# Local attention: ScalarE's two exponentials of a score tile queued behind two copies instead of directly behind the scores

## The reference, cut to what matters

```python
def local_attention(q, k, v):              # window w = 32, 16 heads of 64
    ...                                    # each block of 32 queries sees 64 keys:
    sim = jnp.einsum('bhwie,bhwje->bhwij', bq, bk2) * QK_SCALE
    sim = jnp.where(mask, -jnp.finfo(sim.dtype).max, sim)
    attn = jax.nn.softmax(sim, -1)
    out = jnp.einsum('bhwij,bhwje->bhwie', attn, bv2)

def attn_layer(x, Wqkv, qs, ksc, Wo):
    qkv = x @ Wqkv                         # 128 -> 3 * 1024
    q = l2norm(q) * qs;  k = l2norm(k) * ksc
    q = q * cos * scale + rotate_half(q) * sin * scale
    k = k * cos * inv + rotate_half(k) * sin * inv
    return local_attention(q, k, v) @ Wo

for i in range(6):
    x = attn_layer(shift_tokens(x), ...) + x
    x = ffn_layer(shift_tokens(x), ...) + x    # layer norm, gated gelu, 341 wide
```

## Time and profile before

| | |
|---|---|
| median of 3 runs | 4403.01 us (4397.09 to 4404.81) |
| profiled execution | 4397.26 us, span 4395.5 us |
| PE busy | 4212.1 us, 96% of the span |
| DVE, ACT, POOL busy | 3251.4, 2614.8, 2168.8 us |
| granted TensorE clock, mean | 0.99 |

### The profile page before, as it was taken

How to read it: one execution, slowest core, us unless ns; L and a number is a source line. 1 busy time by engine, 2 the same in 40 slices (tenths; PEclk the granted TensorE clock), 3 DMA queues, 4 the chain that set the end, 5 groups by cost and what they waited for, 6 DMA issues and landing times.

```text
span 4395.5 us, 159359 instructions
## 1 busy us (share of the span) xinstructions
PE 4212.1 (96%) x68360; PEld 2541.8 (58%) x68360; DVE 3251.4 (74%) x5759; ACT 2614.8 (59%) x5346; POOL 2168.8 (49%) x1986
## 2 busy tenths in 40 slices
PE   8999999999799999999999999999999999999998
PEld 4555555555356666556656656656656556656655
DVE  5666666565578887877887877878887877878875
ACT  4545555455366666666666666666666666666664
POOL 0000000000176766766766766766766666766763
PEclk9999999999899999999999999999999999999998
DMA  1000000000111112111121111211122111221112
GB/s 45 4 8 6 8 4 9 6 8 4 41 52 49 52 45 70 52 47 46 51 71 52 49 46 49 70 51 48 51 61 60 45 50 46 64 60 50 50 46 68
DMA packets 141403, 185.95 MB, mean 42 GB/s; under 512 B 32870, under 2 KB 63652, under 8 KB 140708
## 3 DMA queue, kind: packets, MB, share of 16 engines
q1 hardware_dynamic: 140708, 175.76, 14.7%
HBM read 26.76 MB, written 4.19 MB: 7 GB/s over the span
## 4 chain that ended last, share of the span: by engine, by line
PE 69%; issue 2%; ACT 1%; POOL 1%; DVE 1%; DMA 0%; SPq 0%; DVEq 0%; POOLq 0%; ACTq 0%
PE psum L1599 23%; PE psum L1540 9%; PE psum L1616 8%; PE psum L1604 8%; PE psum L1525 6%; PE psum L1637 6%; PE psum L1609 4%; PE psum L1642 3%; PE psum L1562 2%; PE psum L1622 1%; PE psum L1632 0%; ACT pT L1692 0%; ACT oTl L1694 0%; DVE cs L1779 0%; POOL cs L1480 0%
## 5 line engine op out<-in xcount | busy, mean ns | idle before, releaser
L1480 POOL TENSOR_TENSOR cs<-cs 128x512 f32<-128x512 f32 x768 | 975.7, 1276 | 489.8 <-DVE cs L1779 479.8
L1599 PE MATMUL psum<-wqkv,xw 128*128 128x512 f32 x2304 | 1172.6, 608 | 11.4 <-DMA wqkv<-in_wqkv 9.8
L1779 DVE TENSOR_TENSOR cs<-psum,rots 128x1024 f32<-128x1024 f32 x768 | 930.8, 1212 | 202.1 <-PE psum L1599 195.9
L1489 POOL TENSOR_TENSOR qk<-cs,rn 128x512 f32<-128x512 f32 x768 | 776.5, 1042 | 422.0 <-ACT rn L1663 422.0
L1676 ACT ACTIVATE sq<-psum 128x512 f32<-128x512 f32 x768 | 462.2, 602 | 512.6 <-PE psum L1609 178.7
L1508 POOL MEMSET tiled<- 128x128 bf16 x1 | 0.2, 205 | 1168.1 <-POOLq L590 1168.1
L1736 DVE TENSOR_REDUCE ss<-sq 128x8 f32<-128x512 f32 x768 | 519.4, 676 | 12.4 <-ACT sq L1676 0.8
L1604 PEld LDWEIGHTS psum<-ident,qk 128*128 128x128 f32 x3072 | 362.3, 142 | 219.0 <-issue 199.9
L1599 PEld LDWEIGHTS psum<-wqkv,xw 128*128 128x128 f32 x2304 | 370.8, 191 | 174.9 <-issue 132.5
L1540 PEld LDWEIGHTS psum<-pT,vw 64*64 64x64 f32 x18432 | 382.2, 135 | 110.5 <-issue 110.0
L1506 POOL TENSOR_TENSOR probl<-probl,rs 128x512 f32<-128x512 f32 x384 | 392.4, 1043 | 94.8 <-DVE rs L1769 92.5
(11 more groups left out here) (198 smaller groups left out, 6636.0 us busy)
## 6 DMA issues: line engine op xcount, KB each, us to landing
vw<-vl SPq DMA_DIRECT2D x768, 128.0 KB, 2.4
vw<-vl SPq DMA_DIRECT2D x672, 64.0 KB, 2.1
wqkv<-in_wqkv SPq DMA_DIRECT2D x36, 256.0 KB, 4.5
wol<-in_wol SPq DMA_DIRECT2D x6, 512.0 KB, 3.8
xin<-in_x SPq DMA_DIRECT2D x9, 256.0 KB, 2.9
xr<-in_x SPq DMA_DIRECT2D x8, 256.0 KB, 3.1
sums<-sumout SPq DMA_DIRECT2D x8, 256.0 KB, 2.3
cs<-sums SPq DMA_DIRECT2D x8, 256.0 KB, 4.5
```

Of the source, the lines that this page charges most:

```text
L1480: summed_rot.done(nc.gpsimd.tensor_tensor(own, own, halves(cs[:, t % 2, j, 1, :])[:, :, ::-1, :], ALU.add), at)
L1489: rotated.done(nc.gpsimd.tensor_tensor(qk[:, j, :].rearrange("p (h c) -> p h c", c=EL), cs[:, t % 2, j, 0, :].rearrange("p (h c) -> p h c" ...
L1599: last = nc.tensor.matmul(ps[:, :], xw[:, t * P:(t + 1) * P], wqkv[:, col:col + BANK], start=True, stop=True)
L1779: parts.done(V.tensor_tensor(cs[:, t % 2, j, :, :].rearrange("p i (h c) -> p i h c", c=EL), twice, by_head, ALU.mult), at)
```

## The change

A function `behind_copy` rewrites the list of keys for ScalarE alone. It takes the keys `s.t.0` and `s.t.1` out and puts them back behind the second copy (`t`, `pt`, `o` or `v`) that follows. Where an `n`, `w` or `gate` comes first, they are put back ahead of that. The lists of the other engines stay.

```diff
+def behind_copy(order, kinds, copies):
+    out, held, left = [], [], 0
+    for key in order:
+        if key[0] in kinds:
+            held.append(key)
+            left = copies
+            continue
+        if key[0] in ("n", "w", "gate"):
+            out, held = out + held, []
+        out.append(key)
+        if key[0] in ("t", "pt", "o", "v"):
+            left -= 1
+            if left <= 0:
+                out, held = out + held, []
+    return out + held
...
@@ block.scalar
             for it, order in enumerate(ORDERS):
-                for key in order:
+                for key in behind_copy(order, ("s",), 2):
                     read(it, key)
```

## The result

| | before | changed |
|---|---|---|
| median of 4 runs | 4400.05 us | 4479.91 us (4472.49 to 4481.57) |
| ratio | 1 | 1.018 (95% interval 1.0167 to 1.0193) |
| profiled execution, span | 4397.3, 4395.5 us | 4478.9, 4477.1 us |
| granted TensorE clock, mean | 0.99 | 0.99 |

The forecast was 4466 us with a range of 4425 to 4484 and a chance of 0.91 for slower. The changed kernel does the same work: the page counts the same instructions, and PE, DVE and POOL are busy as long as before to within 0.5%. The 80 us are waiting and pauses of PE. The page shows 64 us more idle time (183.4 before, 247.7 now) and 17 us more busy time; the ends of matmuls are modelled late, so a part of each wait counts as busy.

The account below looks back on a forecast made before the run. PE, busy for 96% of the span, was taken as the bound. Tile 0's 68 us, plus 2 for tile 3, less 3 of pauses, gave +67 us on 4397.3: 4464, predicted as 4466 us, range 4425 to 4484.

Parts of the forecast that it names:

- Tile 3: Two copies, v.0.1 and t.0.0, go ahead; first exponential 0.12 us late; cost 0 to 6 us, taken as 2.
- Tile 0: Exponentials 3.2 us late behind square qk.2.0 and copies v.1.1, t.1.0; reciprocal 2.30 us late; 68 us lost in all.
- First wait: PE at pt.0.0 waits 1.3 us for the first half of POOL's product, in two of three trips.
- Second wait: PE at the mask of tile 1 waits for ACT's kTl copy of t.1.3, 0.45 us in the typical trip.
- DVE's sums: DVE's sums wait for ACT's late exponentials: 2.3 us more idle time per trip, about 100 us in all.
- ACT's exponentials: ACT's idle time before its exponentials falls by about 2.5 us per trip, from 283 to some 165 us.
- The waits: PE's loss per trip: 2.55 us less the distance from kTl copy's end to tile 1's mask; together 68 us.
- The issue pauses: In tile 1's scores behind the mask, a semaphore wait lets PE skip issue pauses of 4.5 us; taken as -3.
- The earlier copies of tile 3: They leave about 1 us earlier; their banks go to o.2.1 and qk.1.3, where neither waits; gain 0.
- Rival 1: PE's issue pauses, about 40 us, are paid back by the waits; loss 28 us, 4425 us; chance 0.11.
- rival 2: No cover counts for PE's waits: 48 times 2.30 = 110 us, 4507 us; chance 0.05.
- Rival 3: Earlier copies of tile 3 free banks PE's mask waits on; at most 24.4 us gained, 4373 us; chance 0.04.

Follow-up runs that it names:

- e1: Kernel before, with only tile 3's exponentials put behind v.0.1 and t.0.0, tile 0's left in place: ratio 0.9992, -2.8 us.
- e2: Kernel before, with only tile 0's exponentials put behind qk.2.0, v.1.1 and t.1.0: ratio 1.0178, +79 us.
- e4: Kernel before, with tile 0's exponentials behind the square of qk.2.0 alone, ahead of both copies: ratio 1.0079, +37 us.
- e7: Kernel before, with ACT's copy of t.1.3 moved behind the square of qk.2.2: ratio 1.0093, +39 us.
- e6: Kernel before, with ACT's square of qk.3.1 moved behind the copies of t.2.3, o.0.0 and o.0.1: 4363.65 us, ratio 0.9918.
- e5: Kernel before, with tile 0's exponentials behind t.1.0 and DVE's sums of tile 0 behind the rotary product of qk.2.1: ratio 1.0105, +45.5 us.

## Why the prediction was right, and where its sum was off

**The mechanism held step by step.**
- Tile 3: first exponential 0.12 us late. From PE's start of s.3.0 to it, it was 2.80 us and is 2.91 (4028.52 to 4031.43). Cost: forecast 2 us (0 to 6), measured -2.8 us, with an interval that reaches to no change (e1).
- Tile 0: sums 2.30 us late. From PE's start of s.0.0 to the first sum, it was 4.41 us and is 6.70: 2.29 us.
- First wait 1.3 us: 1.31, in 27 of 47 trips where I had two of three. Second wait 0.45 us: 0.31.
- DVE's sums: 116.7 us of idle time for the forecast "about 100". ACT's exponentials: 186.7 for "some 165". Those of tiles 0 and 3 lost 111 us of idle time (118 forecast), and those of tile 1 gained 13, since the pauses of s.1.0 make them wait.
- The two exponentials together: I had 0.53 us from one start to the next, and the row of 1.17 us for two of 0.64 gives the same 0.53.
- Nothing later in the trip was paid twice, and nothing but tile 0 paid (e1, e2).

**Three terms of the sum were mis-sized.**
- *The waits: 68 forecast, 57 measured over the same 48 trips.* For the handover from ACT's copy to the mask I took 0.25 us from a place of the chain where the mask of tile 2 waits for pT. There it is 0.25 us in the typical trip too. But at tile 1, behind the copy of kTl, the mask of the changed kernel starts 0.14 us after the copy's end. Each trip so has 0.11 us more cover, 5 us in all. Of the other 5 us, 2.7 lie in trips 8, 21, 34 and 47, which had no pause in o.3 before and have one now, and so more cover; the rest is spread over trips with such a pause.
- *The issue pauses: -3 forecast, about +20 measured.* This is the step that failed in sign. I wrote that a wait "can let it skip an 'issue' pause right behind". The runs show the reverse at the scores of tile 1: +18.3 us in the changed kernel, +17.1, +16.9 and +17.2 in e2, e4 and e7, and -8.8 at tile 2 when the wait ahead of it is taken away (e6). What I described does exist: in e5, where PE waits at pt.0.0 and the mask's copy is in time, s.1.0 loses its 4.3 us. It fails where the awaited copy is the one that opens the score tile.
- *The earlier copies of tile 3: nothing forecast, -10.5 us measured in o.2.0, as a part of the +20.* I put the gain at 0 because no PE row waits for those banks. With the copy of v.0.1 2.8 instead of 0.8 us ahead of oa.2 the pauses of o.2.0 went, and 8.8 us came back in s.0.0, so that tile 3 still comes out near nothing.

The time lies 4 us inside the upper end of the range, and that 67 came so near to 80 is luck: the waits, sized 11 us too high, hid half of the 23 us by which the pauses were missed. The last step of the sum is also off. 4464 us for the profiled execution and the median's 5.7 us above it make 4470, and I wrote 4466.

Rival 1, the pauses paid back, didn't come: in all they grew; rival 2 (no cover) had the wrong reason for a larger loss. Rival 3, that earlier copies pay, was rightly put aside for this change, since it moves none of the copies that L1562 waits for. Its price, the 24.4 us, was there to be had all the same: e6 takes it by letting copies pass a square.

## What to carry to other kernels

Idle time in front of an instruction is a place for other work only if that work is ready then. An instruction which brings a wait of its own (here a square that waits for DVE) moves that wait ahead of everything put behind it, and the engine still idles. So look, item by item, at when each thing that goes ahead becomes ready, and at who waits for what goes behind: two copies ahead cost nothing, the same two with one square cost 1.8%. And where a busy PE comes to dense runs of short matmuls, what opens such a run should be ready well ahead: here 0.8 us ahead still left pauses, 1.5 us or more hardly any.

## What the runs showed of the hardware

A late copy costs PE twice: once as a wait, and again as a pause some 2.4 us further on, inside the run of 64 short matmuls, in the trips in which, as I read it, a block of its code ends there. Three things in the traces point to the supply of instructions. The page of the changed kernel has a queue for it,

```profile
q8 instruction: 549, 8.99, 0.8%
```

which is 549 packets of 16.4 KB, 477 of them in the local attention. First, the place of the pause moves by ten matmuls from one trip to the next: in the changed kernel it lies behind the 40th, 50th and 60th of the 64 in trips 1 to 3, then behind the 2nd, 12th and so on to the 62nd in trips 10 to 16. Where it would fall outside the run there is none, hence the 23 trips. Second, of 896 gaps of over 0.25 us inside the score and output runs, in all twelve kernels, 98% end 2.1 to 3.3 us after the start of a q8 packet, though packets are 6.7 us apart on average. Third, in the 141 cases with a pause in s.1.0 the packet ahead of it starts 1.06 to 2.29 us after the end of the copy that the mask needs, and never sooner: the later the copy, the later the fetch.

The Trainium skill, Runtime: NRT & Kernel Launch, section "Instruction fetch mechanics", says that a sequencer refills its store in 16 KiB blocks of 256 instructions by its own DMA queue; the packet size agrees. It also says that the cost is mostly hidden. By count the trace agrees, with 57 pauses in the waits before for 477 packets; what isn't hidden sums to 37 us before and 54 us after, up to 1.8 us each. My reading is that PE's sequencer runs ahead of its array, asks for the next block that much earlier, and loses this lead when a semaphore holds it. The Trainium skill, TensorE: Matmul & The Clock Gate, section "Architectural detail", gives TensorE a queue of 64 instructions, which would be that lead; no run here shows its depth. That a copy which ends late before the mask brings the pauses is shown, by e4, e5 and e7 and by the trips; that the fetch starts late with it is read from the packets; the lost lead as the reason is argued.
